# A transformer with a mixture of experts on one core: prologue and entry rebuilt, and the experts' gate and up projections in three rounded passes

## What is computed

```
mod = silu(c) @ wmod                    # per sequence: sa, ca, ga, sb, cb, gb of 128
h   = layernorm(x) * (1 + ca) + sa
x   = x + ga * encoder(h)               # 4 layers, final layernorm; ga, gb kept away from 0
h   = layernorm(x) * (1 + cb) + sb
x   = x + gb * ffn(h)

encoder: y = sqrt(128) * h + positions; per layer
  h = layernorm(y); q, k, v = h @ Wq, Wk, Wv (+ bias), 16 heads of 8
  y = y + linear_attention(elu(q) + 1, elu(k) + 1, v) @ Wo + bo
  h = layernorm(y); y = y + relu(h @ W1 + b1) @ W2 + b2       # hidden 512
ffn: shared expert (hidden 128) + top 2 of 8 experts (hidden 64 each), each
  silu(h @ gate) * (h @ up) @ down, weighted by the router's softmax
```

## Time and profile before

| | |
|---|---|
| median of 3 runs | 641.19 us (640.11 to 641.77) |
| the profiled execution's own time | 639.92 us |
| its span, first to last instruction | 638.1 us |
| mean granted TensorE clock | 0.984 |
| busy: PE, DVE, ACT, POOL | 583.4, 467.9, 378.0, 265.9 us |
| HBM read, written | 13.07 MB, 2.14 MB |

### The profile page before, as it was taken

How to read it: one execution, slowest core, us unless ns; L and a number is a source line. 1 busy time by engine, 2 the same in 40 slices (tenths; PEclk the granted TensorE clock), 3 DMA queues, 4 the chain that set the end, 5 groups by cost and what they waited for, 6 DMA issues and landing times.

```text
span 638.1 us, 12632 instructions
## 1 busy us (share of the span) xinstructions
PE 583.4 (91%) x4378; PEld 538.3 (84%) x4378; DVE 467.9 (73%) x1440; ACT 378.0 (59%) x1344; POOL 265.9 (42%) x414
## 2 busy tenths in 40 slices
PE   2756999998899999998899999998989999999887
PEld 1255999997799999997798999997888999998776
DVE  5774666668997656669998566668998566668784
ACT  0658556654677566664676656664576665665431
POOL 6157533445443333455543243345442343435210
PEclk9876999999999999999999999999999999999999
DMA  9803400000000000000000000000000000000000
GB/s 278 293 26 99 129 2 1 1 2 2 1 18 18 1 2 2 1 2 0 2 17 18 2 1 1 2 3 0 2 17 2 17 1 2 1 1 2 2 16 18
DMA packets 10527, 16.01 MB, mean 25 GB/s; under 512 B 848, under 2 KB 7580, under 8 KB 10208
## 3 DMA queue, kind: packets, MB, share of 16 engines
q1 hardware_dynamic: 6304, 10.02, 4.9%
q0 software_dynamic: 1008, 2.83, 1.5%
q10 hardware_dynamic: 3152, 2.36, 1.3%
HBM read 13.07 MB, written 2.14 MB: 24 GB/s over the span
## 4 chain that ended last, share of the span: by engine, by line
PE 65%; DVE 15%; ACT 10%; issue 4%; POOL 3%; DMA 2%; DVEq 1%; SPq 0%; POOLq 0%
PE psB L1313 15%; PE psD L1313 15%; PE psA L1313 15%; PE psC L1313 14%; PE psB L1349 2%; DVE xnB L895 1%; DVE H L1051 1%; PE psA L1349 1%; PE psC L1349 1%; ACT eqkB L423 1%; POOL rstdB L662 1%; DMA wm<-in_wmod 1%; ACT L431 1%; DVEq L885 1%; PE psD L1349 1%
## 5 line engine op out<-in xcount | busy, mean ns | idle before, releaser
L662 POOL TENSOR_TENSOR rstdA<-msA,neghalf 128x2 f32<-128x2 f32 x36 | 25.1, 697 | 68.8 <-ACT eqkA L423 64.9
L662 POOL TENSOR_TENSOR rstdB<-msB,neghalf 128x2 f32<-128x2 f32 x36 | 25.1, 698 | 68.6 <-ACT eqkB L423 67.2
L662 POOL TENSOR_TENSOR rstdD<-msD,neghalf 128x2 f32<-128x2 f32 x36 | 24.9, 692 | 64.6 <-ACT eqkD L423 63.4
L662 POOL TENSOR_TENSOR rstdC<-msC,neghalf 128x2 f32<-128x2 f32 x36 | 25.1, 697 | 59.9 <-ACT eqkC L423 52.2
L423 ACT ACTIVATE eqkC<-xC 128x129 f32<-128x129 f32 x64 | 19.4, 304 | 35.3 <-DVE xC L955 35.3
L423 ACT ACTIVATE eqkA<-xA 128x129 f32<-128x129 f32 x64 | 19.3, 303 | 22.0 <-DVE xA L955 22.0
L1313 PE MATMUL psC<-w,H 128*128 128x128 f32 x256 | 31.5, 276 | 0.0
L1313 PE MATMUL psB<-w,H 128*128 128x128 f32 x256 | 31.4, 276 | 0.0
L1313 PE MATMUL psD<-w,H 128*128 128x128 f32 x256 | 31.4, 276 | 0.0
L1313 PE MATMUL psA<-w,H 128*128 128x128 f32 x256 | 31.2, 275 | 0.0
L1313 PEld LDWEIGHTS psC<-w,H 128*128 128x128 f32 x256 | 30.0, 192 | 0.7 <-ACT H L444 0.7
(11 more groups left out here) (503 smaller groups left out, 2338.6 us busy)
## 6 DMA issues: line engine op xcount, KB each, us to landing
M<-modulation_rows SPq DMA_DIRECT2D x1, 2560.0 KB, 11.3
out<-X SPq DMA_DIRECT2D x16, 128.0 KB, 1.9
M<-modulation_rows SPq DMA_DIRECT2D x2, 640.0 KB, 5.1
M<-modulation_rows SPq DMA_DIRECT2D x1, 1280.0 KB, 8.8
M<-in_attn_W ACTq DMA_DIRECT2D x1, 1024.0 KB, 16.0
w<-in_attn_W POOLq DMA_DIRECT2D x1, 1024.0 KB, 11.8
X<-in_attn_x_in ACTq DMA_DIRECT2D x1, 512.0 KB, 4.7
wm<-in_wmod SPq DMA_DIRECT2D x1, 384.0 KB, 6.4
```

What stands on the lines that cost most here:

```text
L662: pool.tensor_tensor(b.rstd[:, :], b.ms[:, :], neghalf[:, :], ALU.pow).then_inc(b.s_rstd.sem, 1)
```

## The change

**Gate and up.** `two` now takes three passes per chunk, with weights split once (`experts_high` on ACT, `experts_low` on POOL, 1280 columns each) and the tokens' low part by DVE:

```diff
-                    last = mm(b.ps[:, bank, j * T:(j + 1) * T], w[:, c, :], b.xT[:, :])
+                    last = exact(b, b.ps[:, bank, j * T:(j + 1) * T], wgu_hi[:, w, c, :], wgu_lo[:, w, c, :])
...
             def gate(b, i, k):
-                if k == 1:
+                if k == 0:
+                    pe.wait_ge(b.s_x_lo.sem, b.s_x_lo.value(i, 2 * LAYERS + 1))
+                elif k == 1:
```

`tokensT` moves from DVE to ACT, where it is two activations (xT and x_hi); `low_part` for n = 8 is new on DVE, from xT in SBUF:

```diff
+            def tokensT(b, i):
+
+                act.wait_ge(b.s_tps.sem, b.s_tps.value(i, 2 * LAYERS + 1))
+                s = seq_of(b, i)
+                act.activation(b.xT, b.ps[:, 0, 0:T], ACT.Identity, scale=scaleT[:, s:s + 1], bias=shiftT[:, s:s + 1])
+                act.activation(b.x_hi[:, :], b.ps[:, 0, 0:T], ACT.Identity, scale=scaleT[:, s:s + 1],
+                               bias=shiftT[:, s:s + 1]).then_inc(b.s_xT.sem, 1)
```

**Entry.** Each chain has two buffers x, used by turns. `stats` for the next step runs in the second layer's phases, `in_shift` and `in_rstd` (POOL) and `in_scale` (DVE) in the third, `in_enter` (DVE) and `centre` (ACT) in the fourth:

```diff
+            def in_scale(b, i):
...
+                for t in range(TILES):
+                    last = dve.scalar_tensor_tensor(b.zi[:, t, :], x_tile(b, i, t), b.in_mv[:, t, 0:1], factor,
+                                                    ALU.subtract, ALU.mult)
+                last.then_inc(b.s_in.sem, 1)
+
+            def in_enter(b, i):
...
+                for t in range(TILES):
+                    last = dve.scalar_tensor_tensor(x(b, i)[:, t, :], b.zi[:, t, :], b.in_rstd[:, t:t + 1],
+                                                    x(b, i)[:, t, :], ALU.mult, ALU.add)
+                last.then_inc(b.s_in.sem, 1)
```

**Exit.** The last scaling and the first `leave` on DVE are gone. POOL multiplies by the row (`gated`), DVE does the rest in one step of two halves:

```diff
+            def gated(b, i):
+
+                rows_there(pool, i)
+                pool.wait_ge(b.s_moved.sem, b.s_moved.value(i, 2 * LAYERS))
+                pool.tensor_tensor(b.z, x(b, i), mod_row(b, i, 2), ALU.mult).then_inc(b.s_mod.sem, 1)
...
+            def leave(b, i):
+
+                dve.wait_ge(b.s_mod.sem, b.s_mod.value(i, 1))
+                dve.wait_ge(b.s_biased.sem, b.s_biased.value(i, LAST))
+                dve.wait_ge(b.s_rstd.sem, b.s_rstd.value(i, LAST))
+                for t in range(TILES):
+                    last = dve.scalar_tensor_tensor(b.y[:, t, :], b.z[:, t, :], b.rstd[:, t:t + 1], b.zi[:, t, :],
+                                                    ALU.mult, ALU.add)
+                last.then_inc(b.s_moved.sem, 1)
```

**Prologue.** The rows of the first four sequences come from matmuls with the condition's column broadcast, straight into each chain's PSUM, where DVE adds the constants:

```diff
+            def first_rows(b):
+
+                pe.wait_ge(s_condT, 2)
+                pe.wait_ge(s_wm, 16)
+                mm(b.ps[:, 0, 0:2 * D], condT_root[:, b.c:b.c + 1].to_broadcast([P, P]), wm[:, 0:2 * D]).then_inc(s_inmod, 1)
...
+            def fold_weights(n):
...
+                mm(b.ps[:, 1, 0:width], fold[:, n, :], w, stop=False)
+                mm(b.ps[:, 1, 0:width], unit[:, :], bias[:, l, first:first + width], start=False).then_inc(s_foldps, 1)
```

```diff
+            parameters()
+            fold_matrix(0)
+            in_stats(D_, 0)
+            in_stats(A, 0)
+            in_stats(B, 0)
+            first_rows(A)
+            in_scale(A, 0)
+            bias_plus_one(0, 1)
+            in_enter(A, 0)
...
+            modulation(1)
+            scale(A, 0, 2)
+            scale(B, 0, 2)
+            fold_matrix(4)
+            fold_matrix(5)
+            fold_matrix(6)
+            fold_matrix(7)
```

More of the change, by code:

```diff
@@ L289, in program @@
         s_foldps = sem("foldps")
-        s_folded = sem("folded")
         s_high = sem("high")
@@ new lines, in _ @@
+            in_scale(C, 0)
+            low(0)
+            in_enter(D_, 0)
+            low_part(A, 0, 0)
+            low(1)
+            modulation(0)
+            scale(B, 0, 1)
+            positive_keys(A, 0, 0)
+            in_enter(C, 0)
+            positive_queries(A, 0, 0)
+            low_part(B, 0, 0)
+            masked(A, 0, 0)
+            less_means(0)
+            positive_keys(B, 0, 0)
+            divided(A, 0, 0)
+            positive_queries(B, 0, 0)
+            masked(B, 0, 0)
@@ new lines, in _ @@
+            bias_plus_one(1, LAYERS)
+            fold_matrix(2)
+            fold_matrix(3)
+            divided(B, 0, 0)
+            less_means(1)
+            low(2)
+            scale(D_, 0, 1)
+            move(A, 0, 1)
+            scale(C, 0, 1)
+            move(B, 0, 1)
+            low(3)
+            less_means(2)
+            modulation(1)
[5 more added lines that the diff above has]
+            fold_matrix(7)
```

2076 lines of the change are left out of this document (1171 added, 905 removed).

## The result

The kernel after takes 631.09 us (median of 4 runs, 627.57 to 635.64), the one before 641.45 beside it: ratio 0.985, 95% interval 0.981 to 0.989. A second set gave 630.13 against 640.68, 0.984 (0.982 to 0.985). So it is 1.6% faster, where 5% was forecast, and it lies 3 us above the forecast's range. Three executions of 981, 2033 and 3204 us are left out; two of them were the profiled ones of a_plain_gates and b_small_entry2, so these two runs have times and no profile. The profiled execution of the kernel after took 631.3 us, its span is 629.5.

What follows compares the result with a forecast made beforehand. PE was taken to limit the layers, DVE and short chains through it to hold PE up in the expert stretch; -13.7 + 6.1 + 3 - 12.8 - 13.2 - 1.5 = -32.1 from 639.92 gave 607.8, median forecast 609 us, range 596 to 628.

Steps and rivals of the forecast that it cites:

- Prologue, -13.7: Before the loop: without the DMA trip VectorE's own list sets the opening, at 41 instead of 54.71, 13.7 us sooner.
- Folds in step 0, +6.1: Step 0: four of eight folds move there, each with a second matmul for the bias, adding 6.1 us.
- Once-only work in step 0, +3: Step 0: 26 us of other once-only work on ACT, POOL and DVE moves there, 3 us of it exposed.
- Gates, -12.8: Expert stretches: three passes cut each of 160 gate chunks from 0.433 to 0.353 us, 12.8 us less on PE.
- Entry and exit, -13.2: Three expert stretches: taking entry work off DVE gives back half of PE's 8.8 us gaps, 4.4 each, 13.2 us.
- rival 1: Expert stretches: PE's gaps stay, belonging to the chain from move to logits and the coefficients; 624 us, chance 0.18.
- Layers, costed at nothing: Layers: the next sequences' entry work on DVE, ACT and POOL has room in the 80 us, no cost charged.
- Rival 5: Layers: moved work stalls PE, which is full there; at 60% of 86 us exposed, slower at 657 us, chance 0.07.
- A row and a rule, costed at nothing: Scalings took 547 ns for B, 417 for A; a rule says DVE and GpSimd lock each other out; no cost charged.
- rival 3: DVE and POOL block each other in new two-input operations, 3.6 us a step on DVE; 616 us, chance 0.05.
- the shorter leave and tokensT: Last step, with no next entry to take out: these give 1.5 us, bounds 0 and 5.

Runs made afterwards that it cites:

- a_plain_gates: The kernel after with each gate and up chunk as one plain float32 matmul in place of three rounded passes: 637.09 us, ratio 0.9940 to the kernel before.
- b_small_entry2: The kernel before with the entry work of steps 2 and 3 on 8 columns in place of 128: 638.69 us, ratio 0.9960.
- a_modulation_later: The kernel after with eight VectorE operations of the modulation's second half moved from the prologue into step 0: 626.61 us, ratio 0.9797 to the kernel before.
- b_three_passes: The kernel before with its 160 gate and up matmuls as three rounded passes on stand-in operands: 644.03 us, ratio 1.0044.
- b_three_keep: The kernel before with three-pass gate and up products and ten unneeded matmuls a step in TensorE's wait before chain D's router transposes: 641.08 us, ratio 1.0005.
- a_plain_again: The kernel after with plain float32 gate and up matmuls, run once more for its profile: 636.11 us, ratio 0.9936 to the kernel before.
- a_small_entry2: The kernel after with the entry work of steps 2 and 3, now in the layers, on 8 columns: 629.23 us, ratio 0.9817 to the kernel before.
- a_bias_order: The kernel after with GpSimd's bias additions and entry shift reordered away from VectorE's scalings, every operation kept: 627.24 us, ratio 0.9788 to the kernel before.
- a_keep_clock2: The kernel after with eight unneeded matmuls a step in TensorE's wait before chain C's first expand of layer 3: 627.90 us, ratio 0.9797 to the kernel before.
- a_all: The kernel after with bias reorder, experts' low part on VectorE, later modulation, chain A's router product earlier and four filler matmuls: 619.01 us, ratio 0.9672 to the kernel before.
- a_logits_first: The kernel after with chain A's router product ahead of chain C's first expand of layer 3: 628.56 us, ratio 0.9808 to the kernel before.
- after_again: The kernel after, unchanged, timed again beside the variants: 630.13 us.

## Why the prediction was wrong, point by point

Against its sum of 607.8 the profiled execution missed by 23.5 us. Three steps failed: that shorter products on PE are worth their full price (4), that half of PE's gaps in the expert stretch belong to the moved entry work (5), and that moved work and the lock cost nothing in the layers (6 and 7). Beside them the clock had no term (8).

1. **Prologue, -13.7: right.** DVE's list did set the opening, and it was busy 29.5 of the first 40 us. The loop opened at 39.48, forecast 41, so 15.2 us sooner; the clock stayed at half of full speed for some 7 us behind the wait there, and by the first contraction 13.5 were left. The match to 0.2 us is partly luck. a_modulation_later shows that 2.6 us more were to be had.
2. **Folds in step 0, +6.1: under-sized.** From start to start a matmul of 384 columns took 0.74 to 0.84 us where 256 columns scaled gave 0.65, one of 512 took 0.96 to 1.05 where they gave 0.87; the four pairs sum to 7.3. This is the pair at 59.87, the second with one row of weights only (the next product starts at 61.88):

```profile
59.87 1.02 PE L1533 MATMUL psD<-M 128*128 128x512 f32 x2
60.83 1.12 PE L1533 MATMUL psD<-M,unit 1*128 1x512 f32 x2
```

3. **Once-only work in step 0, +3: right in size.** Step 0 took 10.2 us more than step 1; less 7.3 that is 2.9. The main piece is one I had not named: the experts' low part on POOL stopped DVE's scaling of D.
4. **Gates, -12.8: the step that failed is "160 x 0.08 us less on PE".** The pitch was right (0.118 and 0.35 for three, at 310.15 to 310.50), the value was not: 1.8 us a step, 6 to 7 in all. I priced the records and took for granted that PE sets the time there, right after writing that DVE holds it up in that stretch. In the old order the passes are worth 0, by b_three_passes and b_three_keep.
5. **Entry and exit, -13.2: the term with the largest miss.** The step was "of these 8.8 us I give back half, 4.4 in each stretch". With plain products the stretch goes from 69.6 (before) to 67.3 (a_plain_again), 2.3. Taking nearly all the entry out of the old order gives 1.2 a stretch by the median (1.7 and 2.3 with three passes, by the profile). So the term was about twice too large, and the rest of the gaps stayed, as rival 1 had all of them stay; I had read DVE's busy share as the cause. That what stayed belongs to the experts' own chain is what is left over, not shown link by link.
6. **Layers, costed at nothing: +2.0 a step.** Rival 5's place at a fraction of its price: 2.0 of the 20 us moved is exposed, 10%. 0.9 of it is the moved work (a_small_entry2). Most of the rest goes with the order in which POOL's bias additions meet DVE's scalings: a_bias_order takes 0.7 to 0.8 us from the layers and 0.9 from the stretch. In the last step, which has no entry work, the layers go from 77.2 to 76.35 with it, where they took 76.3 before. Some 0.3 us a step are unplaced.
7. **A row and a rule, costed at nothing.** The 547 against 417 ns was the warning. The Trainium skill, SBUF — State Buffer, "Who interferes with whom", has a DVE instruction with two SBUF inputs and a GpSimd instruction that reads SBUF shut each other out for a whole instruction. The trace agrees: 0.94 and 2.68 us beside POOL's work, 0.41 alone. By the count in rival 3 the new operations would pay 3.6 us a step, 14 in all; in fact it was mostly the old scalings, moved into POOL's path: 13.5 us more on DVE. Of the new ones, four groups are longer than their like (in_enter of A and C, 488 and 484 ns against 347; in_scale of D, 519 against 346; leave of D, 535 against 348), 4.8 us in all.
8. **The clock** had no term. Against 153.6 for step 0 and 143.5 for the next two, which a_keep_clock2 shows, it took 0.6, 0.6 and 2.1 us.

Added up per their places: 5.6 for the passes (4 x 1.4), 6.3 for the stretches (3 x 2.1), 6.9 for the layers (3 x 2.0 and 0.9), 3.3 for the clock, 1.2 for the folds: 23.3 of 23.5. The layers' 2.0 in step 0 and the passes' 1.8 in the last step aren't measured there but carried over from the steady steps; on them the shorter leave and tokensT gave 3.1 - 1.8 = 1.3 in the last step, forecast 1.5. (The last stretch of a_plain_again, 59.6 against 58.2, would give the passes 1.3 there.)

What stays open: why the clock falls behind the same wait, and near the start, in some executions only, and which link of the experts' chain would have to be shortened for the rest of the 1.4 us a step. No run was made for either.

## What to carry to other kernels

Before a term "PE's work gets shorter" is added, find in the windows who is at its limit while that work runs: with DVE at 7.3 to 7.9 of 8 us, 12.8 us of shorter products were worth nothing, and the longer gap cost 2.9 us more with the fall of the clock. When work is moved between two in-order queues, look at what will run side by side: under a lock the second operation ended some 0.3 us behind the first, however long that was (0.73 or 2.89 us), and a new order of calls, with nothing removed, gave 2.9 us. A run that leaves work out (8.2 us) may have a shorter chain in its price as well; the reorder, which keeps every operation, is the cleaner price of the lock.

## What the runs showed of the hardware that was not expected

- The exclusion works both ways: POOL's rstd on 128x2, 0.70 us as a rule, took 1.19 at 34.64 in a_all, where DVE's subtraction of two SBUF operands had started at 34.59. A DVE scaling beside such an rstd was not lengthened (0.41 at 236.04, rstd of C at 235.91, in the kernel after; so in all 33 cases there).
- A float32 matmul of 512 columns with one row of weights was no shorter than one with 128 rows: the next product started 1.05 us later, in place of 0.96 (60.83 and 59.87 in the kernel after).
- Behind a plain float32 product of 256 columns a rounded one starts after 0.028 us in place of 0.216, but the one behind that only after 0.305 in place of 0.118 (27 times in a_plain_again): nothing is gained or lost.
- TensorE's clock fell to its lower level behind waits of 1.76 us (b_three_passes), 1.42 (the kernel after) and even 0.60 and 0.21 (a_logits_first). Behind the same waits it doesn't always fall: the kernel after lost 2.1 us so in step 2 of its first profile and nothing in that of after_again. With 10 and 8 matmuls put into the wait it was at 1.00 there in the profiled executions of b_three_keep and a_keep_clock2.
